# Two VectorE operands of a two-layer graph network, kept in PSUM instead of SBUF

## The reference

```python
# layer 0: attention over the edges, softmax per destination node
rel_t = abs(last_update[src] - t)
edge_attr = concatenate([msg, cos(rel_t[:, None] * time_w + time_b)], -1)
h = x @ Wx.T + bx
q, k, v = h @ Wq.T + bq, h @ Wk.T + bk, h @ Wv.T + bv
e = edge_attr @ We.T
alpha = sum(q[dst] * (k[src] + e), -1) / sqrt(128)
alpha = exp(alpha - segment_max(alpha, dst)[dst])
m = segment_sum((v[src] + e) * (alpha / (segment_sum(alpha, dst)[dst] + 1e-16))[:, None], dst)
h = tanh(h + tanh(h @ A.T + m + b_ac))
x = layernorm(x + h)
# layer 1: message network over the edges, then a node network
edge_new = relu(concatenate([x[src], x[dst]], -1) @ We1 + be1) @ We2 + be2
x = layernorm(x + x + mlp(concatenate([x, segment_sum(edge_new, dst)], -1)))
```

## Time and profile before

| what | value |
| --- | --- |
| median of the three runs | 6106.25 us |
| profiled execution, first to last instruction (span) | 4307.4 us |
| profiled execution's own time | the page gives no other than its span |
| median of the runs less the span | 1798.9 us |
| gathers in layer 0 | 1563, from 61.7 us on |
| gathers in layer 1 | 1563, from 2239.3 us on |
| GpSimd, busy | 3084.2 us, 72% of the span |
| VectorE, busy | 2081.9 us, 48% |
| TensorE matmul, busy | 3331.1 us, 77% |

### The profile page before, as it was taken

The page is one execution under the profiler, slowest core; times in us unless marked ns, Lnnn a source line. Parts: engine busy times, 40 slices in busy tenths (PEclk is TensorE's granted clock), DMA queues, the critical chain, the costliest instruction groups (busy, mean ns, idle before and its releaser), DMA issues. The chain is left out here.

```text
span 4307.4 us, 84038 instructions
## 1 busy us (share of the span) xinstructions
PE 3331.1 (77%) x25735; PEld 3093.0 (72%) x25735; DVE 2081.9 (48%) x5360; ACT 1729.2 (40%) x2766; POOL 3084.2 (72%) x3188
## 2 busy tenths in 40 slices
PE   6887888788888878788667777777777777777777
PEld 3877788778878777787547777667776676777674
DVE  3777777676767676767472222222222222222223
ACT  3655555555555555555352222222222222222223
POOL 5777777777777777777247777777777777777771
PEclk9999999999999999999888888887788888888888
DMA  6333333333333333333232222222222222222221
GB/s 169 75 74 73 75 73 74 73 75 73 75 73 75 73 75 73 75 73 75 63 90 58 57 57 57 57 57 57 56 57 57 56 57 57 57 57 56 57 56 44
DMA packets 398441, 292.85 MB, mean 68 GB/s; under 512 B 266467, under 2 KB 341755, under 8 KB 398300
## 3 DMA queue, kind: packets, MB, share of 16 engines
q0 software_dynamic: 100032, 205.87, 20.0%
q1 hardware_dynamic: 289948, 81.55, 8.5%
q10 hardware_dynamic: 8386, 4.57, 0.4%
HBM read 271.33 MB, written 20.32 MB: 68 GB/s over the span
## 5 line engine op out<-in xcount | busy, mean ns | idle before, releaser
L622 POOL DMA_INDIRECT he<-h_table,src_i x1563 | 1528.6, 978 | 487.5 <-issue 475.7
L1316 POOL DMA_INDIRECT msg<-p_table,src x1563 | 1509.1, 966 | 485.5 <-issue 475.9
L1429 DVE TENSOR_TENSOR msg<-msg,p_edge 128x512 f32<-128x512 f32 x392 | 251.8, 683 | 1450.8 <-DMA msg<-p_table,src 1450.8
L1348 PE MATMUL p_edge<-r_win,hotT 80*128 80x128 f32 x3136 | 523.0, 335 | 498.8 <-DVE msg L1429 498.8
L1348 PEld LDWEIGHTS p_edge<-r_win,hotT 80*128 80x128 f32 x3136 | 479.5, 241 | 537.2 <-issue 536.8
L1393 ACT ACTIVATE msg<-msg 128x1024 f32<-128x1024 f32 x196 | 207.2, 1057 | 1136.8 <-DVE msg L1429 1049.7
L1359 PEld LDWEIGHTS p_sum<-hot,msg 128*128 128x128 f32 x3136 | 469.7, 237 | 3.9 <-issue 1.1
L1359 PE MATMUL p_sum<-hot,msg 128*128 128x80 f32 x3136 | 467.4, 314 | 0.8 <-DVE acc L1441 0.8
L667 PE MATMUL p_score<-qk_win,heT 128*128 128x80 f32 x3136 | 446.2, 265 | 0.0
L667 PEld LDWEIGHTS p_score<-qk_win,heT 128*128 128x128 f32 x3136 | 432.3, 191 | 0.0
L734 ACT ACTIVATE rest<-feat 128x256 f32<-128x256 f32 x196 | 92.9, 474 | 800.6 <-DVE rest L810 800.6
(11 more groups left out here) (173 smaller groups left out, 4777.5 us busy)
## 6 DMA issues: line engine op xcount, KB each, us to landing
feat<-in_edge_attr_dram SPq DMA_DIRECT2D x196, 128.0 KB
he<-h_table,src_i POOLq DMA_INDIRECT x1563
msg<-p_table,src POOLq DMA_INDIRECT x1563
qk_win<-qk_table SPq DMA_DIRECT2D x196, 40.0 KB
qk_two<-qk_table SPq DMA_DIRECT2D x392, 20.0 KB
r_win<-r_table SPq DMA_DIRECT2D x196, 40.0 KB
qk_table<-qk SPq DMA_DIRECT2D x13, 512.0 KB, 3.3
h_table<-h_rows ACTq DMA_DIRECT2D x13, 258.0 KB, 3.9
```

The costliest lines, as they stand in the source:

```text
L622: e.indirect_dma_start(out=he[u][:, j, 0:ROW], out_offset=None, in_=h_table[:, :], in_offset=bass.IndirectOffsetOnAxis(ap=src_i[u][:, j:j ...
L1316: e.indirect_dma_start(out=msg[u][:, j, :], out_offset=None, in_=p_table[:, :], in_offset=bass.IndirectOffsetOnAxis(ap=src_i[u][:, j:j + 1 ...
L1348: mm = e.matmul(p_edge[h][:, j % 4, :], hotT[:, j * P:(j + 1) * P], r_win[u][:, :], start=True, stop=True)
```

## The change

`level` no longer is a tile of its own in SBUF but the first 80 columns of `p_turn[3]` in PSUM; lines 881 and 885 write and read it there. Before the loop of the first round VectorE waits for all copies out of `p_turn[3]`. In layer 1 a PSUM tile `p_iota` is added, filled once by a copy of `iota_row`, and line 1419 compares with it. Empty lines at the head of the file are dropped, so line numbers after the change are lower.

```diff
-            level = sb("level", [P, W], ctx=ctx)
...
+            level = p_turn[3][:, 0:W]
...
-                            e.tensor_tensor(level[:, :], top[:, :], p_qbk, ALU.subtract).then_inc(level_done, 1)
+                            e.tensor_tensor(level, top[:, :], p_qbk, ALU.subtract).then_inc(level_done, 1)
...
-                            e.tensor_tensor(prob[:, :, :], score[:, :, :], level[:, :].unsqueeze(1).broadcast_to([P, J, W]),
+                            e.tensor_tensor(prob[:, :, :], score[:, :, :], level.unsqueeze(1).broadcast_to([P, J, W]),
                                             ALU.subtract).then_inc(below_done, 1)
...
                             pipelined(e, (1, copy_k1))
+                            e.wait_ge(k2_done, NG)
...
+            p_iota = ctx.enter_context(nc.psum_tensor("p_iota", [P, W], F32))
...
+            iota_done = sem("iota_done")
...
-                                            iota_row[:, :].unsqueeze(1).broadcast_to([P, J, W]), ALU.is_equal).then_inc(hot_done, 1)
+                                            p_iota[:, :].unsqueeze(1).broadcast_to([P, J, W]), ALU.is_equal).then_inc(hot_done, 1)
...
+                        if at_first:
+                            e.tensor_copy(p_iota[:, :], iota_row[:, :]).then_inc(iota_done, 1)
+                            e.wait_ge(iota_done, 1)
                         hots((0, 0))
```

## The result

The changed kernel takes 6159.9 us (median of 5 runs, 6144.02 to 6179.45), the kernel before 6110.33 us (median of 5, 6098.81 to 6116.34), timed together with it. The ratio is 1.0074, 95% interval 1.0049 to 1.0099: **slower by 0.7%**. The forecast was 6070 us, -0.6%, and its range ended at 6125.

What follows compares the result with a forecast made beforehand. The prediction took GpSimd's pitch of gathers to bound both edge loops. Layer 0's -16 us and layer 1's -20.5 us made -36 us, taken from 6106.25 us to give 6070 us (-0.6%), range 6020 to 6125 us.

Steps and rivals of the forecast that it cites:

- I take this part as unchanged: Whole kernel: the 1798.9 us by which runs exceed the profiled span, place unknown, would stay as they are.
- Rival E: Both layers' gathers: runs paced unlike the trace, missing time 0.58 us per gather; 6106 us, or 5836 if hit; chance 0.10.
- What bounds the kernel, the holds and their rule: Both edge loops: GpSimd's gather pitch sets the time; two-SBUF-input VectorE instructions hold gathers until their end + 0.82 us.
- Line 1419, -20.5 us: Layer 1 compare: the 83 gathers it holds go free, nothing takes over; 20.5 us gained, bounds 15 and 21.
- What is late next: line 834, +23 us: Layer 0: line 834 newly holds gathers, 29 us less about 6 it causes already; of 38.8 us freed, 16 remain.
- rival B: Layer 0: every chunk becomes early and all its gain is given back; -20.5 us, 6086 us; chance 0.12.
- The early kind: Layer 0 chunks with line 834 under 7.3 us after line 797, 118 of 182: 0.23 us new delay each, 29 us.
- The late kind: The other 64 of 182 layer 0 chunks: moved gathers miss line 834, so the saving stays.
- Durations from PSUM, 825 ns: Lines 885 and 1419: still 825 ns each with a PSUM operand, bounds -10 and +70 ns.
- The wait for `k2_done`, the copy into `p_iota`: One-off costs: the wait hidden, else 0.8 us once; the copy about 0.2 us once, hidden too.
- Rival C: Both layers: gathers are held whatever the operand's place, so the change frees none; 0 gain, 6106 us; chance 0.12.
- Rival D: Layer 0: line 834 hits harder than both lines did; slower, up to +62 us, 6168, likelier 6125; chance 0.12.

Runs made afterwards that it cites:

- iota only: Kernel before with only layer 1's compare (line 1419) reading its counting row from PSUM: 4289.56 us, 0.9961 on chip P; 6042.62 us, 1.0008 on chip S.
- the control: Changed kernel with its wait, PSUM tile and copy kept, but lines 885 and 1419 reading SBUF: 6034.75 us, 0.9985 against the kernel before on chip S.

## Why the prediction was wrong, point by point

- *"I take this part as unchanged"*, the 1798.9 us between span and runs. **This is the step that failed.** There is no such part: each timed run's span is 1.8 us shorter than its time. The 1798.9 us are the difference between two kinds of chip, and the sum was made on the one and added to the median of the other. On the chips of the timed runs GpSimd stands 1183.0 + 689.6 us for indices in the changed kernel, so the 36 us taken off the gathers aren't on the path. The table ahead of the prediction gave cause to stop: 1798.9 us is 42% of the span, too much to be left without a name, and the question "what would this kernel look like if it really took 6100 us" has another bound (GpSimd waiting for indices, all engines late) as its answer.
- *Rival E* said so much and had 0.10. Its premise held, its prices did not: it put the missing time onto the gathers (0.58 us each) and saw only gains or nothing. It had no way in which the change could cost time.
- *What bounds the kernel, the holds and their rule.* Right for chips P and Q: 885 holds 188 gathers there, and with one PSUM operand none.
- *Line 1419, -20.5 us.* Right on P (4309.8 to 4289.56; mean of the gathers 964 to 952 ns). Nothing on S, where those gathers aren't on the path.
- *What is late next: line 834, +23 us.* The mechanism was right, the term mis-sized. 834 held 146 to 153 gathers for 44 us, where 32 for 7 us were before: +37. Layer 0 gains 37.9 - 37 = 1 us: rival B, which had 0.12, and B has every chunk turn early, which didn't happen. The early kind cost what the forecast said, 30.0 us for 130 gathers against 127 x 0.23 = 29. The late kind, put at no delay, held 24 for 14.6 us, as at 1012.61; and the "about 6" taken off for what 834 holds already (9.3 us in that trace) was not to be taken off in the late chunks.
- *Durations from PSUM, 825 ns.* Right within its bounds: 821. The Trainium skill's rule (VectorE: DVE Perf Modes, "The TRN2 errata"), 65 ns more for a PSUM source, would have made 890; no trace here shows it.
- *The wait for `k2_done`, the copy into `p_iota`.* Right: 0.8 us once, and the control with both costs nothing (0.9985).
- *Rival C* (no hold to free) is refuted by the gathers that 885 and 1419 no longer hold on chip P, and by "iota only". *Rival D* had the right sign for the result and the wrong mechanism: line 834 pays back just about what 885 gave, on P.

What is shown: on chip S the loss is `level`'s, in layer 0, and of the size of the longer standstills at 20 places, where GpSimd often makes 15 gathers in one stretch; a pause in every chunk takes 3% off the kernel before on chip T. What is argued only: that the pause works by breaking the stream of gathers; and that gathers held less make layer 0 longer, which the order of the kernels on each chip agrees with. What the traces don't bear out: that it is 885's hold in the chunk ahead of a place that keeps the standstill short. What is open: by what step `level` in PSUM makes the standstills longer, why instructions come late on some chips and not on P and Q, why the places are nine chunks apart, and whether the change costs nothing with a pause there.

## What to carry to other kernels

Before a sum is made on a trace, hold its span against the timed runs; if they differ by more than a few us, the trace is of another regime, and its bound need not be the bound of what is measured. An engine that isn't the bound may be worth slowing: on chip T a pause after each chunk's gathers took 3% off, but on Q, where the gathers are the bound, pauses cost 6.5 to 11%, so measure on both kinds. Where a hold is freed, count again for the whole pattern who holds next: the phases move with it.

## What the runs showed of the hardware

- One program takes 4310 us on two chips and 6040 to 6140 us on three others, with busy times of VectorE, ScalarE and GpSimd that agree within 2%. On the latter TensorE's matmuls of one line often start 0.70 or 1.40 us after one another (392 and 205 of the 1247 distances of over 450 ns on chip R); those distances add up to 1341 us, where chip P has 25 us. The granted clock differs with it: between 1000 and 2000 us, in layer 0, it is 0.74 in the changed kernel, with the matmuls busy 69% of the time, and 0.97, nearly all at the upper level of 2.4 GHz, in the kernel before on chip P with 80%.
- A gather whose look-up, 0.126 us after its start, falls into a 640-wide VectorE instruction with two SBUF inputs ends 0.82 us after that instruction. With one input in PSUM it isn't held: 188 held gathers went to none on chip P.
- A wait of GpSimd on its own fill costs 0.54 us beyond the fill, for 8 elements as for 512 (0.84 us to the next gather instead of 0.30, chip Q).
- A 640-wide float32 `tensor_tensor` takes 815 to 821 ns with one input in PSUM and 820 to 826 ns with both in SBUF.
